# Feed-forward low halves all on VectorE, and three PSUM places for up projections

## The reference, cut to what matters

```python
shared = silu(xf @ Ws_up) @ Ws_down
aff = xf @ centroids.T                       # 64 experts
_, idx = top_k(aff + expert_biases, 8)
w = sigmoid(take_along_axis(aff, idx, 1));  w = w / (sum(w) + 1e-8)
h = silu(einsum('td,edf->etf', xf, W_up))    # every expert, F = 64
y = einsum('etf,efd->etd', h, W_down)
return shared + einsum('etd,te->td', y, cw)  # cw: w at idx, else 0
```

## Time and profile before

| | us |
|---|---|
| median of 3 runs (1105.13 to 1108.87) | 1106.67 |
| profiled execution | 1106.26 |
| its span | 1104.3 |
| TensorE busy in the span | 1006.7 |
| DVE busy | 958.2 |
| ACT busy | 891.8 |
| Pool busy | 520.5 |

### The profile page before, as it was taken

How to read it: one execution, slowest core, us unless ns; L and a number is a source line. 1 busy time by engine, 2 the same in 40 slices (tenths; PEclk the granted TensorE clock), 3 DMA queues, 4 the chain that set the end, 5 groups by cost and what they waited for, 6 DMA issues and landing times.

```text
span 1104.3 us, 21657 instructions
## 1 busy us (share of the span) xinstructions
PE 1006.7 (91%) x8016; PEld 516.2 (47%) x8016; DVE 958.2 (87%) x1170; ACT 891.8 (81%) x1466; POOL 520.5 (47%) x909
## 2 busy tenths in 40 slices
PE   6389999999999999999999989998899899989998
PEld 3022222222222222222222337776678777867886
DVE  7799999999999999999999747888767977777675
ACT  5179999999999999999999977766676776678775
POOL 3353546455645564556455665354325542443331
PEclk9579999999999999999999999999999999999999
DMA  8901110111011101110110037665467466857774
GB/s 283 302 27 41 52 50 16 37 51 50 13 40 51 50 15 38 52 50 16 37 52 21 4 67 186 154 150 126 117 175 189 118 174 154 195 130 174 189 196 103
DMA packets 80472, 108.91 MB, mean 99 GB/s; under 512 B 23536, under 2 KB 33520, under 8 KB 80368
## 3 DMA queue, kind: packets, MB, share of 16 engines
q1 hardware_dynamic: 66336, 100.98, 34.7%
q10 hardware_dynamic: 14032, 6.55, 2.3%
HBM read 95.57 MB, written 11.93 MB: 97 GB/s over the span
## 4 chain that ended last, share of the span: by engine, by line
DVE 58%; PE 25%; ACT 6%; issue 5%; DMA 5%; SPq 1%; POOL 0%; ACTq 0%; DVEq 0%
DVE NEGMAX L1058 47%; PE PS L1450 6%; PE PS L1452 6%; PE PS L1451 6%; DVE HF L1099 3%; DMA GATE<-gate_d 3%; DVE XC L1005 2%; PE PS L1352 2%; DVE HL L1107 2%; ACT PS L948 2%; ACT PR L853 1%; PE PS L1325 1%; ACT L948 1%; DVE ln_st L993 1%; ACT HH L941 1%
## 5 line engine op out<-in xcount | busy, mean ns | idle before, releaser
L1058 DVE TENSOR_REDUCE NEGMAX<-PS 128x1 f32<-128x1024 f32 x512 | 584.8, 1210 | 10.0 <-PE PS L1288 9.4
L853 ACT ACTIVATE PR<-PS 128x512 f32<-128x512 f32 x1024 | 539.0, 601 | 37.4 <-PE PS L1325 24.9
L1352 PE MATMUL PS<-PR,VG 128*32 128x256 f32 (+1 forms) x3840 | 322.1, 407 | 17.1 <-ACT PR L853 1.8
L1325 PE MATMUL PS<-QB,KB 32*128 32x512 bf16 x1024 | 260.5, 388 | 3.2 <-DMA QB<-shift_d 1.9
L1099 DVE TENSOR_TENSOR HF<-PS,GATE 128x1024 f32<-128x1024 f32 x128 | 156.0, 1221 | 89.9 <-ACT PS L948 82.8
L1288 PE MATMUL PS<-KA,QA 32*128 32x512 bf16 x1024 | 204.8, 398 | 30.7 <-DVE NEGMAX L1058 22.6
L948 ACT ACTIVATE PS<-PS 128x1024 f32<-128x1024 f32 x128 | 129.2, 1009 | 89.5 <-PE PS L1452 88.4
L1325 PEld LDWEIGHTS PS<-QB,KB 32*128 32x128 bf16 x1024 | 75.1, 91 | 239.7 <-ACT PR L853 138.5
L765 POOL TENSOR_TENSOR HL<-HF,HH 128x1024 fp32r<-128x1024 f32 (+1 forms) x48 | 108.9, 2268 | 160.7 <-ACT HH L941 160.4
L941 ACT ACTIVATE HH<-HF 128x1024 fp32r<-128x1024 f32 (+1 forms) x136 | 139.7, 1028 | 35.0 <-DVE HF L1099 34.1
L1352 PEld LDWEIGHTS PS<-PR,VG 128*32 128x32 f32 x3840 | 76.5, 108 | 130.8 <-issue 64.6
(11 more groups left out here) (186 smaller groups left out, 985.8 us busy)
## 6 DMA issues: line engine op xcount, KB each, us to landing
GATE<-gate_d SPq DMA_DIRECT2D x256, 256.0 KB, 4.1
QA<-q_stack SPq DMA_DIRECT2D x64, 128.0 KB, 2.6
QB<-q_stack SPq DMA_DIRECT2D x16, 256.0 KB, 3.0
KB<-k_stack SPq DMA_DIRECT2D x16, 256.0 KB, 3.0
KA<-k_stack SPq DMA_DIRECT2D x60, 64.0 KB, 2.4
q_stack<-PARTS SPq DMA_DIRECT2D x12, 256.0 KB, 4.3
k_stack<-PARTS SPq DMA_DIRECT2D x12, 256.0 KB, 4.0
RAWU<-in_L_ffn_W_up_dram ACTq DMA_DIRECT2D x4, 512.0 KB, 10.8
```

Source lines behind the costliest of these rows:

```text
L853: nc.scalar.activation(PR[:, s % PRING, r, :], PS[:, SCORE_BANK[n], :], ACT.Exp, scale=SCALE_A).then_inc(p_ready, 1)
L1058: nc.vector.tensor_reduce(NEGMAX[:, hs % 2, col:col + 1], PS[:, e:e + 2, :].rearrange("p b n -> p (b n)"), axis=AX_X, op=ALU.max, negate=T ...
L1325: mm(PS[:, SCORE_BANK[n], :], KB[strip, u, mt * P:(mt + 1) * P], QB[strip, u, half * BANK:(half + 1) * BANK], start=True, stop=True).then_ ...
L1352: last = mm(PS[STRIP * r:STRIP * (r + 1), 7, cols], VG[:, u, mt, r // 2, :], PR[:, s % PRING, r, cols], start=mt == 0, stop=mt == TB - 1 a ...
```

## The change

ZSLOTS goes from 2 to 3: three PSUM places of two banks for `up`, banks 0 to 5. That leaves bank 6 for the sums of `down` and bank 7 for all side items, each with one bank where there were two; `down` of a chunk waits for the chunk sum of the chunk before, a side item for the evacuation of the item before. The last output tile moves to bank 6, and TensorE waits for its evacuation at step 3 instead of 2. `low_on_pool` returns False: all 136 low halves are DVE's. ACT copies an affinity and takes its sigmoid behind `high(g - 1)` instead of ahead of it. In the attention's last quads gate_T of chunk 0 stands a quad earlier, DVE takes the +1 and the reciprocal ahead of the maxima, and copies the last output tile ahead of the first gated product instead of behind it. x_T of b 0 moves from step (1, 10) to (1, 11).

```diff
-ZSLOTS = 2
+ZSLOTS = 3
...
-    NQ - 8: [("x_T", ("f", 0))], NQ - 7: [("affinity", 0)], NQ - 6: [("top", 0)], NQ - 5: [("sum", 0)], NQ - 2: [("gate_T", 0)],
+    NQ - 8: [("x_T", ("f", 0))], NQ - 7: [("affinity", 0)], NQ - 6: [("top", 0)], NQ - 5: [("sum", 0)], NQ - 3: [("gate_T", 0)],
...
-    (1, 10): [("heads_T", 3), ("x_T", ("b", 0))], (1, 11): [("top", 2)], (1, 12): [("proj", 3), ("stats", ("f", 3))],
+    (1, 10): [("heads_T", 3)], (1, 11): [("x_T", ("b", 0)), ("top", 2)], (1, 12): [("proj", 3), ("stats", ("f", 3))],
...
 def low_on_pool(g):
 
-    here = divmod(g + 1, WIDES)
-    if not POOL_BUSY <= g < 2 * NCH * WIDES - 5:
-        return False
-    if works(here, ("affinity",)):
-        return True
-    return not works(here, POOL_SIDE) and (works(here, DVE_SIDE) or here[1] % 3 == 0)
+    return False
...
+TAIL_BANK, DOWN_BANK, SIDE_BANK = 1, 6, 7
...
+    bank[TILE["out", 2 * NG - 1]] = DOWN_BANK
...
-TAIL_BANK, SIDE_BANKS, DOWN_BANKS = 1, (6, 7), (4, 5)
...
-    return TAIL_BANK if n < TAIL_ITEMS else SIDE_BANKS[n % 2]
+    return TAIL_BANK if SIDE_ITEM[item] < TAIL_ITEMS else SIDE_BANK
...
-    return SIDE_ORDER[n - 1] if 0 < n <= TAIL_ITEMS else SIDE_ORDER[n - 2] if n >= TAIL_ITEMS + 2 else None
+    return SIDE_ORDER[n - 1] if n else None
...
                 if g > 1:
                     silu(g)
-                side((n, w), True)
                 if g:
                     high(g - 1)
+                side((n, w), True)
...
                     elif stage == "top":
 
+                        if isinstance(where, int):
+                            dve.wait_ge(ex_ok, arg + 1)
+                            link(nc.vector.tensor_scalar(EX, EX, 1.0, None, ALU.add))
+                            link(nc.vector.reciprocal(EX, EX))
                         dve.wait_ge(bi_ok, arg + 1)
...
-                        if isinstance(where, int):
-                            dve.wait_ge(ex_ok, arg + 1)
-                            link(nc.vector.tensor_scalar(EX, EX, 1.0, None, ALU.add))
-                            link(nc.vector.reciprocal(EX, EX))
...
             evac_out(DVE_OUT + 1)
+            copy_out(DVE_OUT + 1)
             for g in range(2 * NCH * WIDES):
...
                     gated(g)
-                if g == 0:
-                    copy_out(DVE_OUT + 1)
...
-                if w == 0 and n >= 2:
-                    pe.wait_ge(y_evac, n - 1)
+                if w == 0 and n:
+                    pe.wait_ge(y_evac, n)
...
-                    last = split3(PS[:, DOWN_BANKS[n % 2], :], wh, wl, HH[:, k, u, :], HL[:, k, u, :], j == 0, w == FULL)
+                    last = split3(PS[:, DOWN_BANK, :], wh, wl, HH[:, k, u, :], HL[:, k, u, :], j == 0, w == FULL)
...
-                if g == 2:
+                if g == LAG:
                     pe.wait_ge(out_ok, 2 * NG)
```

More of the change, by code:

```diff
@@ L273 @@
 SCORE_BANK, TILE_BEFORE = score_banks()
-TAIL_BANK, SIDE_BANKS, DOWN_BANKS = 1, (6, 7), (4, 5)
 def side_bank(item):
-    n = SIDE_ITEM[item]
-    return TAIL_BANK if n < TAIL_ITEMS else SIDE_BANKS[n % 2]
+    return TAIL_BANK if SIDE_ITEM[item] < TAIL_ITEMS else SIDE_BANK
 def bank_before(item):
     n = SIDE_ITEM[item]
-    return SIDE_ORDER[n - 1] if 0 < n <= TAIL_ITEMS else SIDE_ORDER[n - 2] if n >= TAIL_ITEMS + 2 else None
+    return SIDE_ORDER[n - 1] if n else None
 def chunk_of(key):
@@ L957, in chunk_sum @@
                 act.wait_ge(down_ok, (n + 1) * WIDES)
-                nc.scalar.activation(YS[:], PS[:, DOWN_BANKS[n % 2], :], ACT.Copy).then_inc(y_evac, 1)
+                nc.scalar.activation(YS[:], PS[:, DOWN_BANK, :], ACT.Copy).then_inc(y_evac, 1)
             for s in range(NQ):
```

## The result

The changed kernel takes 1100.29 us (median of six runs, 1097.27 to 1100.72) beside 1107.01 for the kernel before on the same chip. The ratio is 0.9933 with a 95% interval of 0.9915 to 0.9951; it leaves out one slow run of the kernel before, of 1464.94 us, which the median counts. That is 6.7 us faster by the medians and 7.4 by the ratio: the sign and the range hold, the gain is 40 to 44% of the forecast.

What follows compares the result with a forecast made beforehand. TensorE sets the pace, with 34.4 us of waits and slow clock to win; less 15.8 lateness, 2.5 and 1.5 for single banks leaves 14.6, plus 2.2 at the start: 16.8 off 1106.3, 1089.5 (median 1090), range 1076 to 1103.

Steps and rivals of the forecast that it cites:

- The start: Attention's last quads: gate_T a quad earlier and the last output tile copied sooner bring the first `down` forward, gaining 2.2 us.
- The loads on each engine: All low halves moved from Pool to DVE: DVE's net load grows by 29.9 us, norm instructions fall from 806 ns to 0.26 us.
- the row that spoke against the change: A small Pool step took 1.28 us beside a DVE low half; roots held so could cost up to 20, taken as 0.
- the lateness: DVE falling behind in bursts of side work in the first seven passes: peaks less 1.9 slack leave 15.8 us of stalls.
- That stays: ACT's table reloads and sigmoid delay silu, leaving DVE idle 4.07 us; claimed unchanged, as ACT's work is the same in either order.
- the 34.4: TensorE's recoverable time in us: 25.0 of waits, 4.6 hidden in them, 4.8 from half clock after long waits.
- One bank for `down`: At chunk borders `down` waits for ACT's chunk sum: seven times 0.7 is 4.9 us, half taken, 2.5.
- One bank for side items: A side item waits for the previous one's evacuation: 4.5 us at affinity copies, plus chained residuals; 1.5 taken for both.
- Three places: Three PSUM places for `up` free its wait on gated products, but LAG stays 3: worth only about 0.2 us by themselves.
- (B): Rival: DVE becomes the bound in crowded passes, including seven waits of 4.1 for ACT's reloads; 1099 us, chance 0.21.
- (A): Rival: three places decouple more than allowed, so the stalls nearly vanish; 1070 us, chance 0.14.
- (C): Rival: slower, single banks tie TensorE to evacuations queued behind DVE's low halves; 1116 us, chance 0.09.

## Why the forecast was right in sign and too large

**The start** held: 2.5 us (1.2 to 3.8) for 2.2.

**The loads on each engine** held: DVE 30.5 more for 29.9, no wait for Pool's low halves. The norm's tensor_scalar came down to 363 ns, not 260 to 280. Eleven small steps of roots were held to over 1 us beside a low half of DVE, as many as before; they kept one norm waiting, for 0.9 us, so the row that spoke against the change cost nearly the 0 that I took. What I had not looked at is how Pool's own work holds low halves on DVE: eleven of them take 1.36 to 2.96 us instead of 1.22, each beside an elementwise instruction on Pool.

**The step that failed is the lateness**, "15.8 us of stalls left". With two places and double banks, where only it is at work, it was 15.8 + 0.2 = 16.0; measured are 19.7 us in 22 waits, 23.4 with the hidden part, and 1.4 for seven slow pitches, 24.8. The count of DVE's side work was not too low: with the loads gone 11.3 us of waits are left. The fault was to let an affinity lift the lateness to "2.8", as one item among the others, with a later burst as the pass's peak. The loads hold silu, `high` and, through them, the low half, so TensorE is stopped at `up` and again at `down`, before DVE's next burst. The earlier trace rows had shown DVE idle 4.07 at such a place (the trace of before has six such waits, 4.07 to 6.18 us and 30.6 in all, not seven of 4.1). I wrote "That stays" and took them into the sum only by that 2.8, instead of asking how much of the 34.4 they were. In the changed kernels the loads are worth 12.1 to 14.2 us of time.

**One bank for `down`**, "2.5", was sized too low as a wait: its seven waits hold 8.9 shown, 10.1 with the hidden part. The price of a border by itself, 0.7, was right (0.5 or less shown, once the loads are gone); that ACT comes to three of seven chunk sums behind a table load was not in it. **One bank for side items**, "1.5": 4.5 for the affinity's copy, exactly the amount that I had worked out before I lowered it to 1.5, and 1.6 for a residual. But part of both takes the place of other waits: single banks cost 2.6 to 4.2 us of time and 1.5 to 2.0 of stretch, so my 4.0 for the two was not too low.

**Three places**, "worth only about 0.2": by the medians minus 0.6 to minus 2.0 in time, not clear of noise, and about minus 3 in the stretch. That `down` stays due at LAG 3 was right. The clock I had wrong: the sum counts all its cost, 4.8 (by the count of 20 pitches 4.0), as won, with "no slow clock near the norms". Long waits remained at other places, and 19 slow pitches, 3.8 us, with them.

In the sum of the stretch: lateness and clock, 16.0, became 24.8, 8.8 more; single banks, 4.0, became 1.5 to 2.0; the third place, a gain of 0.2, became a loss of about 3. That takes 9.5 to 10.0 us off the 14.6 and leaves 4.6 to 5.1. Measured are 3.5, and 4.7 in the repeat of the changed kernel (436.26 less 431.55).

**The rivals.** (B) hit the time, 1099, but not by its mechanism: DVE is busy 84% and 88% of the crowded passes, under the 95% that was to show it, and taking work off ACT alone gave 12 to 14 us. Its term for the seven waits on ACT's loads was the right one to look at. (A) would have needed the stalls to vanish; 27.2 us stand. (C) is out: side items wait 4.0 + 1.4 + 0.8 us, under the 10 that were its sign.

**Open.** Whether `high` ahead of the affinity's copy is worth anything with two places was not run apart: the two kernels that differ by it, and by the start and the moved x_T, have stretches of 425.86 and 427.17, 1.3 apart, about what two profiles of one kernel differ by. The clock's part was not taken away by itself; it rests on the count of slow pitches, which differs between executions. And no run took the table loads out of the kernel before, so what part of its 34.4 they were is not shown.

## What to carry to other kernels

Where an engine is late, first list what it does that is no work: two table loads for a 0.42 us sigmoid cost 1.7 to 2.0 us each time, and another function of the set already loaded (tanh beside silu) took them away. A buffer more in front of a consumer whose due time stays moved the wait downstream here and took none away; price it together with what it takes the room from. A cover that holds where its engine is on time is no cover behind that engine's longest stop: look at each border and ask what stood before it.

## What the hardware showed that I had not expected

- tanh follows silu and silu tanh with no table load (fence above); sigmoid needs one of 1.28 us each way.
- Half clock behind a long wait of TensorE is not certain: it followed 20 of 31 waits of 2.0 us or more and none of 40 between 1.2 and 1.6. The same wait of 2.05 at the same border was followed by it in one profile and not in the next.
- A reciprocal of 128x256 on DVE takes 1.75 us, more than a 128x1024 product at 1.22.
- DVE's low halves can be held beside Pool's elementwise work, as its norms were: eleven of the changed kernel's took 1.36 to 2.96 us instead of 1.22, and all eleven ran beside such an instruction. Some 20 others that met one took 1.22.
- The same kernel's first `down` came 3 us apart in two profiles, while the 430 us behind it agreed within 1.2. A gain at the start can't be read from one profile of each kernel.
